# Projecting half of the batches inside the first scan of a gated state-space and sparse-layer kernel

## The reference, cut to what matters

```python
# block 1, for each of 4 batches b; the 1024 channels e go over 1024 steps l
x_e  = in_proj_w @ ctx[b].T                      # 1024 x 512 by 512 x 1024
u    = silu(causal_conv4(x_e) + conv_b)          # depthwise, 4 taps
dt, B, C = split(x_proj_w @ u, (32, 16, 16))
delta = softplus(dt_proj_w @ dt + dt_proj_b)
state[e, n] = state[e, n] * exp(delta * A[e, n]) + delta * u * B[n]   # over l, 16 states
y    = sum_n state * C[n] + D * u
x2   = x + tanh(g0) * y * silu(layernorm(x))
# block 2
score = layernorm(x2) @ w_router ; pick the 128 best tokens of each batch
out  = x2 + tanh(g1) * layernorm(x2), and for the picked tokens also attention and a gated MLP
```

## Time and profile before

| | |
|---|---|
| median of 3 runs | 3162.67 us (3158.97 to 3163.16) |
| profiled execution | 3152.81 us, its span 3151.1 us |
| PE busy | 77% of the span |
| DVE busy | 69% |
| POOL busy | 53% |
| ACT busy | 41% |
| project, scan 0, route 0, layer 0 begin at | 0, 295.3, 1149.4, 1236.9 us |
| scan 1, route 2, layer 2 | from 1500.7 us to the end |

### The profile page before, as it was taken

The page is one execution under the profiler, slowest core; times in us unless marked ns, Lnnn a source line. Parts: engine busy times, 40 slices in busy tenths (PEclk is TensorE's granted clock), DMA queues, the critical chain, the costliest instruction groups (busy, mean ns, idle before and its releaser), DMA issues. The chain is left out here.

```text
span 3151.1 us, 30288 instructions
## 1 busy us (share of the span) xinstructions
PE 2432.4 (77%) x10552; PEld 1700.3 (54%) x10552; DVE 2176.0 (69%) x2674; ACT 1288.0 (41%) x2311; POOL 1668.0 (53%) x601
## 2 busy tenths in 40 slices
PE   8996667666666632998488888888887179999998
PEld 3332555554545521854366676665554166658863
DVE  5664999999999985331599999999997832410000
ACT  4555555555555522131456555555543211510000
POOL 0001999999999941000688988899996000000000
PEclk9998677777777765999699998899998589999999
DMA  7545314114141134423623632633531564044443
GB/s 283 191 186 202 89 40 148 41 41 149 47 135 55 37 124 185 127 87 98 213 85 99 208 101 80 204 105 109 185 101 60 211 211 134 15 147 151 151 152 107
DMA packets 198094, 401.37 MB, mean 127 GB/s; under 512 B 16960, under 2 KB 85056, under 8 KB 192832
## 3 DMA queue, kind: packets, MB, share of 16 engines
q1 hardware_dynamic: 186752, 343.43, 34.8%
q10 hardware_dynamic: 9856, 51.38, 4.0%
q0 software_dynamic: 1344, 4.72, 0.4%
HBM read 323.98 MB, written 75.50 MB: 127 GB/s over the span
## 5 line engine op out<-in xcount | busy, mean ns | idle before, releaser
L531 POOL TENSOR_TENSOR s_x<-s_du,s_bB 128x2048 f32<-128x2048 f32 x256 | 1156.9, 4533 | 116.6 <-PE s_py L592 93.6
L592 PE MATMUL s_py<-s_ident,s_x 128*128 128x128 f32 x4096 | 668.4, 322 | 363.9 <-DVE s_x L808 351.7
L592 PEld LDWEIGHTS s_py<-s_ident,s_x 128*128 128x128 f32 x4096 | 583.2, 169 | 535.5 <-DVE s_x L808 431.8
L773 ACT ACTIVATE s_pA<-s_delta,s_negA 128x512 f32<-128x512 f32 x1024 | 666.1, 680 | 388.0 <-DVE s_x L808 381.7
L823 DVE TENSOR_TENSOR_SCAN s_pA<-s_pA,s_x 128x512 f32<-128x512 f32 x384 | 452.4, 1214 | 66.9 <-POOL s_x L531 46.7
L823 DVE TENSOR_TENSOR_SCAN s_pA<-s_pA,s_carry,s_x 128x512 f32<-128x512 f32 x384 | 471.6, 1270 | 0.1
L808 DVE TENSOR_TENSOR s_x<-s_pA,s_bC 128x1024 f32<-128x1024 f32 x384 | 461.9, 1203 | 1.0 <-DMA s_bC<-scratch_xd 0.9
L1324 PE MATMUL l_p<-l_hT,l_ring 128*128 128x256 f32 x1792 | 396.7, 380 | 1.8 <-ACT l_hT L1428 1.0
L1324 PEld LDWEIGHTS l_p<-l_hT,l_ring 128*128 128x128 f32 x1792 | 341.7, 191 | 49.5 <-issue 1.4
L538 POOL TENSOR_TENSOR s_x<-s_hp,s_bC 128x1024 f32<-128x1024 f32 x128 | 301.6, 2356 | 12.0 <-DVE s_hp L823 12.0
L1292 POOL TENSOR_TENSOR l_squares<-l_squares,l_minus_half 128x1 f32<-128x1 f32 x4 | 2.2, 554 | 494.6 <-DVE l_squares L1583 494.6
(11 more groups left out here) (177 smaller groups left out, 3034.8 us busy)
## 6 DMA issues: line engine op xcount, KB each, us to landing
scratch_ug<-p_ug ACTq DMA_DIRECT2D x32, 1024.0 KB, 3.9
s_bB<-scratch_xd SPq DMA_DIRECT2D x32, 1024.0 KB, 13.1
s_bC<-scratch_xd SPq DMA_DIRECT2D x32, 1024.0 KB, 14.0
p_xz<-in_x SPq DMA_DIRECT2D x32, 512.0 KB, 3.5
s_u<-scratch_ug SPq DMA_DIRECT2D x64, 256.0 KB, 3.6
s_gy<-scratch_ug SPq DMA_DIRECT2D x64, 256.0 KB, 4.2
s_xt<-in_x SPq DMA_DIRECT2D x64, 256.0 KB, 4.6
scratch_x<-s_xt SPq DMA_DIRECT2D x64, 256.0 KB, 4.3
```

The costliest lines, as they stand in the source:

```text
L531: pool.tensor_tensor(out=x[:, 4 * g:4 * g + 4], in0=du[:, s % 2:s % 2 + 1].broadcast_to([P, 4, HALF]), in1=bB[:, 4 * g:4 * g + 4], op=ALU. ...
L592: last = nc.tensor.matmul(py[:, a], x[:, n, a * P:(a + 1) * P], ident[:], is_transpose=True, start=False, stop=is_last and a == HALF // P - 1)
L773: nc.scalar.activation(pA[:, n % 4], delta[:, s % 2], ACT.Exp, scale=negA[:, s % NE, n:n + 1]).then_inc(dA_ready, 1)
```

## The change

1. `Kept` holds `bB`, `bC`, `dt`, `u`, `ssm`, `w_dt`, `negA`, `diagD`, `ident`, `tg` outside the stages. `project_stage` does 16 steps, for batches 0 and 1 alone. The gates of all four batches stay in it: each step now takes two x tiles (statistics, ACT's L188, and a store of its own for the late gate). At its end SP loads the first B, C, dt and u of scan 0 into them, behind its last x load, which waits until four gates before it are done; `tg`, `ssm`, `w_dt`, `diagD` and `ident` are loaded or made there once.
2. `scan 0` (`early`) projects batches 2 and 3, a unit at a time: 4 matmuls of 512 columns in slots 0 to 3, 4 more with diagonal weights for the 4 taps of the unit before in slots 4 to 7, ACT copies between (`copy_raw` in pair 0, `copy_pre` in pair 4, `make_taps` in pair 2 of the first 8 units), and a store of the convolution before silu (`pre`).
3. `route 0` (`late`) loads `pre`, does silu on ACT, the sums for dt, B, C on PE, and stores u. Five buffers; a load waits until the tile of five before is stored and summed. PE's order is `x_dbl` 0 to 7, `spread(0)`, `x_dbl` 8 to 15, then L1005.
4. `layer 0` has `SLOTS_W` = 6 and loads scan 1's first B, C, dt, u in its weight stream.
5. Both scans start with B, C, constants in place. `gate` stands in pair 2 of scan 1, and in pair 1 of scan 0 as before.

```diff
+class Kept:
+    def load_units(self, sp, t, b, sem):
+        for e in range(2):
+            sp.dma_start(self.u[:, e], t["ug"][(b * NE + e) * P:(b * NE + e + 1) * P, 0:HALF]).then_inc(sem, 16)
+    def load_chunk(self, sp, t, b, sem):
+        sp.dma_start(self.dt[:, 0], t["xd"][b * ND:b * ND + NR, 0:HALF]).then_inc(sem, 16)
+        for g in range(NS // 4):
+            for dst, at in ((self.bB, b * ND + NR + 4 * g), (self.bC, b * ND + NR + NS + 4 * g)):
+                sp.dma_start(dst[:, 4 * g:4 * g + 4], t["xd"][at:at + 4, 0:HALF].partition_broadcast(P)).then_inc(sem, 16)
...
@@ project_stage, SP @@
+            for n in range(4, 2 * STEPS_NOW):
+                load_x(n)
...
+            keep.load_units(sp, t, 0, kept)
+            sp.wait_ge(xd_out, 32)
+            keep.load_chunk(sp, t, 0, kept)
+            sp.wait_ge(kept, 16 * KEPT_LOADS)
@@ project_stage, ACT, in each of 16 steps @@
+                gate(2 * k, ug[:, j, 1])
+                at_least(act, late_out[j], 16 * (k // 2))
+                gate(2 * k + 1, late_gate[:, j])
@@ scan_stage @@
-GATE_AT, ADD_AT, TURN_AT, DT_AT = 1, 1, 3, 5
+GATE_AT, ADD_AT, TURN_AT, DT_AT = (1, 2), 1, 3, 5
+RAW_AT, PRE_AT, TAP_AT = 0, 4, 2
+            def late_projection(s, i):
...
+                last = nc.tensor.matmul(p_in[:], w_in[:, s % 2, i], ctxT[:, chunk(s) % 2, i], start=i == 0, stop=i == NK - 1)
+            def late_convolution(s, i):
...
+                last = nc.tensor.matmul(p_conv[:], diagC[:, s % NE, i], raw[:, s % 2, i:i + HALF], start=i == 0, stop=i == TAPS - 1)
...
+                    if early and at < NK:
+                        late_projection(s, at)
+                    elif early and s:
+                        late_convolution(s - 1, at - NK)
+            if early:
+                for i in range(TAPS):
+                    late_convolution(UNITS - 1, i)
             add_x(UNITS - 1)
...
+                    if early and i == RAW_AT and s:
+                        copy_raw(s - 1)
+                    if early and i == PRE_AT and s >= 2:
+                        copy_pre(s - 2)
+                    if early and i == TAP_AT and s < NE:
+                        make_taps(s)
...
-                    if i == GATE_AT and s:
+                    if i == GATE_AT[fill] and s:
                         gate(s - 1)
@@ route_stage 0: PE, then ACT, then SP @@
+                for k in range(NE):
+                    x_dbl(k)
             spread(0)
+            if late:
+                for k in range(NE, SPAN * NE):
+                    x_dbl(k)
...
+                if late and b == 0:
+                    finish_u(NE + a)
...
+                if k >= LATE_BUFS:
+                    sp.wait_ge(u_out[j], 16 * (k // LATE_BUFS))
+                    sp.wait_ge(xd_sums, k - LATE_BUFS + 1)
+                sp.dma_start(u[:, j], t["pre"][k * P:(k + 1) * P, :]).then_inc(pre_in[j], 16)
@@ layer_stage 0, SP @@
+    SLOTS_W = 8 if last_half else 6
+                if n == T_V and not last_half:
+                    keep.load_units(sp, t, SPAN, kept)
+                    keep.load_chunk(sp, t, SPAN, kept)
```

More of the change, by code:

```diff
@@ L38 @@
 RMS_EPS = 1e-6
+SPAN = 2
+ROWS = SPAN * TOPK
+KT = DI // P
 class Chain:
@@ L107, in load_x @@
[L107 to L114, removed]
-            for j in range(2):
-                sp.wait_ge(ug_out[j], 16 * STEPS // 2 + 16)
+            load_x(2)
@@ L162, in _ @@
[L162 to L166, removed]
+            pe.wait_ge(w_in_ready, 16)
+            for k in range(STEPS_NOW):
+                b, e = k // NE, k % NE
+                at_least(pe, first_tap, k - 1)
+                if k == 2:
+                    pe.wait_ge(w_in_rest, 16)
+                if k == NE:
+                    pe.wait_ge(ctx_in, 16)
+                for h in range(H2):
+                    if k == 0:
+                        pe.wait_ge(ctx_first[h], 16)
+                    for c in range(NK):
+                        last = nc.tensor.matmul(halves(ps[k % 2], h), w_in[:, c, e * P:(e + 1) * P],
+                                                ctxT[:, b * NK + c, h * HALF:(h + 1) * HALF], start=c == 0, stop=c == NK - 1)
+                last.then_inc(projected, 1)
+                if k == 0:
+                    pe.wait_ge(weights, 32)
+                else:
+                    x_dbl(k - 1)
@@ L205, in batch @@
-            def batch(b, is_first):
-                for e in range(NE):
-                    step(b, e)
-                    if e == 0 and not is_first:
-                        copy_out(b - 1)
-            batch(0, True)
-            with act.Fori(1, NB) as b:
-                batch(b, False)
-            copy_out(NB - 1)
+                act.dma_start(t["ug"][k * P:(k + 1) * P, :], ug[:, j].rearrange("p g l -> p (g l)")).then_inc(ug_out[j], 16)
+                if k == NE:
+                    copy_out(0)
+                    act.wait_ge(small, 48)
+                    act.wait_ge(made, 2)
+                    nc.scalar.activation(keep.tg[:], keep.tg[:], ACT.Tanh).then_inc(kept_chain, 1)
+                    for i in range(NE):
+                        last = nc.scalar.activation(keep.diagD[:, i], keep.ident[:], ACT.Copy, scale=keep.ssm[:, i, NS + 1:NS + 2])
+                    last.then_inc(kept_chain, 1)
@@ L308, in scan_stage @@
     pm = bank("pm", [P, HALF])
[L310 removed]
+    act_chain = sem("act_chain")
     dt_in = [sem(f"dt_in{j}") for j in range(2)]
```

498 lines of the change are left out of this document (315 added, 183 removed).

## The result

The changed kernel takes 3100.72 us (median of 4 runs, 3096.7 to 3103.7), the kernel before 3161.19 us in the same session (3158.97 to 3163.16): a ratio of 0.9822 with a 95% interval of 0.9808 to 0.9837, so 56 us faster by the ratio. That is inside the range of 3005 to 3130 and 34 us above the forecast of 3067. The time also lies outside the forecast's own band of 3040 to 3095. The profiled execution has a span of 3102.0 us, 49.1 less than the one before. The one of the kernel before (3152.81 us) is 8 us faster than its median here and that of the changed kernel 3 us slower than its own, so some 11 us of the shortfall that they show is scatter.

A forecast was written before the change was run, and what follows sets the result against it. PE was taken to bound the projection and DVE the first scan. Terms -122 + 8 + 18 + 6 - 6 = -96 took 3152.8 to 3056.8; 9.9 for the median gave 3067 us, range 3005 to 3130.

The forecast's parts named there:

- Rival 1: Second scan and ranking stage: the later gate is free and the transfers hide; 3009 us, chance 0.22.
- rival 3: First scan: PE becomes the bound if its clock stays at 0.74; 29.7 us a unit, 3182 us, chance 0.06.
- rival 2: Second scan: gaps from the later gate make PE start units at a lower clock; +54 us, 3121 us, chance 0.16.
- rival 4: Moved work does not hide: projection gains, first scan and ranking stage give back half; 3111 us, chance 0.08.
- signs of being wrong: First scan over 27 us a unit, kept loads ending later than 180 us, or second-scan gates under 27.2 us apart.
- the sign of 27: First scan: a unit of over 27 us would show the forecast wrong.
- with 20.6 I take a third: 32 x 0.3 = +10: First scan's units: PE's 20.6 us of full-clock work in 25.8 costs DVE gate waits; +10 us, between 0 and 40.
- PE's clock above 0.85 there: First scan: PE's clock share expected above 0.85, with gates 25.8 to 26.3 us apart.
- Projection, -122: Projection stage: sixteen steps go and it ends with the kept loads at 173 us instead of 295.3; -122 us.
- First layer stage, +6: First layer stage: 8.9 MB more takes 30 us, of which six tiles ahead of PE cover 23; +6, 0 to 12.
- Start of the second scan, -19: Second scan's start: data in place -4, MLP weights going first -14, small B waits -1; -19 us.
- Units of the second scan, +13: Second scan's units: 33 us of gate waits go, DVE waits 46 us for ACT at pair 5; +13, -33 to +60.

The follow-up runs named there:

- experiment 7: Changed kernel with PE's ranking-stage order altered: first spread ahead of x_dbl(5), sums, positions and second spread ahead of x_dbl(12); 3089.94 us, ratio 0.9779 to the kernel before.
- Experiment 3: Changed kernel with the second scan's copy of x2 behind the exps of pair 5 instead of pair 4; 3081.93 us, ratio 0.9779 to the kernel before.
- experiment 4: Changed kernel with the second scan's gate back in pair 1; 3078.52 us, ratio 0.9763 to the kernel before.
- experiment 2: Changed kernel with three more matmuls, their results overwritten, in slot 4 of the first scan, taps still in slots 4 to 7; 3073.7 us, ratio 0.9738.
- experiment 6: Changed kernel with the projection stage's kept loads issued between the x loads from the 24th on; 3094.25 us, ratio 0.9802 to the kernel before.
- experiment 11: experiment 8 without experiment 6; only the first quad of B and C is kept, the scan issues the other six loads; 3022.26 us, ratio 0.9581.
- experiment 5: Changed kernel with the first layer stage's kept loads behind the second tile of wo instead of the first of wv; 3085.87 us, ratio 0.9788.
- experiment 8: Changed kernel with the first scan's taps all in slot 4 plus Experiment 3, experiment 5, experiment 6 and experiment 7; 3028.78 us, ratio 0.9588.

## Why the prediction was right and wrong

**Right.** The direction and the kind of each term: every part that was to cost something did, and the two last stages changed by 2.6 us only. The projection's compute ended at about 156 us (forecast 160.5), its last x load was issued at 136.8 (forecast 135). DVE's first scan came 12.0 us after the start of the stage (12), the first gate 8.1 us sooner after it than before (8). The ranking stage's sums came at 72.1 us (75), and experiment 7 shows that the order was the cause of 9.5 of the 15.9 us. In the second scan, the waits moved from the gate to pair 5's exps, with ACT waiting for `add_x`. DVE's waits for the exps are 44.9 us (38.4 and 6.5), where the forecast had 31 x 1.5 = 46. Experiment 3 takes the wait at pair 5 away, and experiment 4 turns the exps' waits back into waits at the gate. Rival 1, the free gate, and rival 3, PE as a bound that makes the whole slower, are out. Of rival 2, a fall of PE's clock in the second scan, little is seen: 0.89 for 0.92, and `skip` at a mean of 299 ns a record for 276.

**Luck in it.** The time is inside the range because the range took in rivals 1, 2 and 4; it is outside the band of 3040 to 3095 that the forecast itself had, and one of the forecast's signs of being wrong came true: the kept loads ended later than 180 us, at 183. The first scan's unit, 26.86, lies above the expected 25.8 to 26.3 and just under the sign of 27. The result lies 10 us from rival 4's 3111, nearer than to the forecast's 3067, and the first scan gave back 32 us where that rival had 38. Its mechanism, that the moved work does not hide at all, is not what the experiments show: with the same work in the same stages, experiment 2 gets 27 us back by the clock (by the ratios) and experiment 7 9.5 us of its stage by order. (Rival 4's time is not the middle that it is said to be; between 3067 and 3182 that is 3125.)

**The step that failed: "with 20.6 I take a third: 32 x 0.3 = +10".** It measured +31.4, inside its own bounds of 0 to 40 but 21 of the 47 us that the forecast was short by the profiled executions (34 by the medians). The step priced the new work by its sum at full clock, 20.6 in 25.8 us, and left PE's clock to one figure for the stage, "PE's clock above 0.85 there". That figure came true (0.88) and said nothing. What counted was where in the unit PE is at the lower level: behind the 3.46 us wait for pair 6, just where slots 5 to 7 and the gate depend on it. There the taps, dt and sums took up to twice their time. The tap record's mean over 226 to 1006 us is 808 ns, 605 in experiment 2. Rival 3 had the right mechanism at too coarse a grain: it asked whether the whole unit would be PE's, not whether its last three slots would.

The Trainium skill's page "TensorE: Matmul & The Clock Gate", section "HAM oscillation — how this bites in real kernels", warns of bursts with waits between them; the prediction cited it for the second scan, and this trace and experiment 2 bear it out for the first.

**Terms of the right kind and the wrong size.**
- Projection, -122: it measured -112.2. The kept loads ended at 183 for 173 (bounds 165 to 179), where the step took them as 30 us of their own behind 8 to 11 us of stores. Until 100 us the steps are PE's (busy 69.65 of 70 us), but the DMA engines are already at 0.91:

```profile
30.00:100.00 70.00, 69.65 (x173) 27.49 (x172) 56.77 (x121) 48.14 (x51) 9.24 (x17) 1.00 0.91 326
```

  So the end of the stage is set by its bytes. Experiments 6 and 11 show it from both sides: earlier loads push other transfers back and gain 7 us, fewer loads start the scan 21 us earlier.
- First layer stage, +6: it measured +12.9, just outside the bounds of 0 to 12. Six tiles of 3.9 us were taken as cover; PE waited 10.2 us. Behind `wo` the loads cost nothing (experiment 5).
- Start of the second scan, -19: at the same place in the unit it is 19.5 (experiment 4). The stage's measured -15.2 is less because the forecast forgot that a gate one pair later is 4.3 us later the first time as well.
- Units of the second scan, +13: +20, inside the bounds.

**Where it went.** The change took 112 us out of the projection and gave 63 back. Experiments 8 and 11 are 74 and 76 us faster than the changed kernel by the ratios (2.3 to 2.4% of the kernel before). Against the kernel before, experiment 8 has the projection at -117.4 us, the first scan at +5.7, the ranking stage at +5.5, the first layer stage at -1.3 and the second scan at -11.1. So little of what the change gave back was necessary. The sum of the two best halves, experiment 11 with the added matmuls and `conv` ahead of B and C, was not run.

## What to carry to other kernels

Work given to an engine that is "only 66% busy" lands in particular slots. Ask of each slot whether something waits right behind it, and what the engine did before it: here TensorE took up to double the time for what followed its longest wait (2.08 us for 1.02). Put movable matmuls in front of what PE waits for anyway, and do not take them from the slots behind it without looking at the next wait. And loads that are "kept" for the next stage need a place where the queue and the engines have nothing due.

## What the runs showed that was not expected

Adding 2.7 us of useless matmuls to every 26 us unit made the kernel 0.84% faster (ratios 0.9738 and 0.9822) and brought the granted clock over 226 to 1006 us of the first scan from 0.88 to 0.97. The same records took 1.02 us at the higher level and 2.08 us behind a wait of 3.46 us, 1.13 us behind one of 0.89.
